# Second attention: transposes of the weights in two halves of 64 tokens

## The chip, the core and the metric

One core of a Trainium2 chip runs one program: two layers of gated cross attention and feed-forward (the second with 8 experts), on 2 x 1024 tokens of 256 channels in 32-bit floats, with 77 context keys. The metric is the device time of one execution in microseconds (us). TensorE (PE) multiplies and transposes and writes to PSUM, in 8 banks of 512 floats per partition; its weight loads are a row of their own (PEld). VectorE (DVE), ScalarE (ACT) and GpSimd (POOL) work beside it, and the engines wait for each other on semaphores.

## The reference

Of the reference the second attention matters here (16 heads of 16 channels, 77 keys; the second input is the context):

```
def _L1_xattn_ref(query, key, value, key_padding_mask, Wq, bq, Wk, bk, Wv, bv, Wo, bo, logit_scale, bias_table):
    ...
    q = proj(query, Wq, bq)
    k = proj(key, Wk, bk)
    v = proj(value, Wv, bv)
    ...
    scores = jnp.einsum('bhqd,bhkd->bhqk', q, k) * scale[None, :, None, None]
    scores = scores + _rel_bias(bias_table, tq, tk)[None]
    scores = jnp.where(key_padding_mask[:, None, None, :], neg, scores)
    attn = jax.nn.softmax(scores, axis=-1)
    out = jnp.einsum('bhqk,bhkd->bhqd', attn, v)
    ...
    out = out @ Wo + bo
    return out
```

Around it stand the first attention, a quantised feed-forward, and the expert layer; each result is added to x with a gate.

## The kernel before

The 2048 tokens are 16 tiles of 128. The second attention goes over them in pairs of tiles: t is the first tile of a pair, u (0 or 1) the tile in it, ci (0 or 1) the half of the heads (8 each). The order of each engine's work is written out by hand; nothing schedules it. Waits are on semaphores counted up by the other engines.

What TensorE does for a pair t, in `pair` of the `@block.tensor` section, is listed here with the names that the profile shows:

- `fill(t, ci)`: scores of 8 heads for both tiles into the four banks of `quad`. It is 16 products on four groups of 32 rows of the array (line 1657, `quad<-k_blockdiag,big_g`, 32x154). It waits for VectorE to be done with the scores before (`e_sub`).
- `weightsT(t, ci, u)`: takes the exponentials `e_` of 8 heads of one tile (in `big_g`) and transposes them, so that keys lie on partitions. Per head it is one transpose of 128 tokens x 77 keys (line 1950, `bank<-ident,big_g`, 128*77, 128x128: the weights are the exponentials, 128 rows and 77 columns, and the 128 columns of the identity are streamed). The first 4 heads go to bank 6, the other 4 to bank 7. Before the first four it waits for the exponentials (`e_exp`), and that ScalarE has copied out bank 6 of the call before; before the other four, that it has copied bank 7 (`pT_sb` counts the copies). A call follows another after one block of other work.
- `token_back(t - 2, u)`: 4 transposes of the heads' output back to tokens on partitions (line 1966, `heads_out`); `project_in`: 4 transposes of the attended tokens (line 1974); `project`: 8 products with the output weights (line 1657, `wo`); `queries(t + 2)`: 8 products (line 1657, `wq`).
- `heads(t, ci)`: 16 products of the values with the transposed weights `pT` (in `big_u`), on four column groups of 32 (line 1657, `bank<-big_u,v`, 77*32, 77x256). It waits for all copies of both tiles.

ScalarE copies each bank out (line 765, `big_u<-bank`, 77x512), so two copies of 512 elements a partition per call; it also makes the exponentials (line 990, in place) and copies queries (line 947), attended tokens (line 985) and `heads_out` (line 765). VectorE takes the maximum and subtracts it (lines 1487, 1488), for each ci and u; in the pairs near the diagonal of the distance bias (`t % TB == TB - NEAR`, t = 6 and 14) it first adds a bias (line 1485). It then makes `att` (lines 1453, 1454), adds the residual (1460) and takes its moments (1468 to 1474).

`PLACES` says where in `pT` each group of 4 heads lies. With ci = 0 these are groups 0 and 2, with ci = 1 groups 1 and 3. Bank 5 holds `oT`, bank 4 queries and projections, and bank 5 or 6 the output of `token_back`.

Of the kernel before, what the change touches and what calls it, by code (L numbers as in the profile page):

```python
# [17 lines left out]
P = 128  # L18
# [3 lines left out]
KEYS = 77  # L22
CH = D // P
H, HD = 16, 16
HK = H * KEYS
HQ = 4
HQK = HQ * KEYS
NQ = H // HQ
HC = H // CH
HCK = HC * KEYS  # L30
# [211 lines left out]
def flamingo_kernel(nc, a, out):  # L242
    ctx = ExitStack()
    with ctx:
        def sb(name, shape, dt=F32):
            return ctx.enter_context(nc.sbuf_tensor(name, shape, dt))
# [6 lines left out]
        pb = [quad[:, i, :] for i in range(4)] + [b[:, :] for b in bank]  # L253
# [15 lines left out]
        def part(reg, off, shape, dt=F32):  # L269

            n = int(np.prod(shape[1:]))
            words = n if dt in (F32, I32) else n // 2
            v = reg[0:shape[0], off:off + words]
            if dt != F32:
                v = v.bitcast(dt)
            if len(shape) == 3:
                v = v.rearrange("p (a b) -> p a b", a=shape[1])
            if len(shape) == 4:
                v = v.rearrange("p (a b c) -> p a b c", a=shape[1], b=shape[2])
            return v  # L280


        ident = sb("ident", [P, P])
# [7 lines left out]
        half = sb("half", [E, 1])  # L291
# [104 lines left out]
        e_ = part(BIGG, 8192, [P, 2, HK])  # L396
# [3 lines left out]
        pT = part(BIGU, 8192, [KEYS, H, 2 * P])  # L400
# [59 lines left out]

        LAST = NT - 2
        PLACES = (0, 2, 1, 3)

        def position(t):

            return t // TB * TB + (t - NEAR) % TB
# [19 lines left out]
        s = Signals(sem)  # L486
# [272 lines left out]
        def _(act):  # L759
            c = Chain(act, s.act_step)  # L760

            def copy(out_, in_, ready, n, done, **k):

                act.wait_ge(ready, n)
                act.activation(out_, in_, ACT.Copy, **k).then_inc(done, 1)  # L765
# [206 lines left out]


            def weightsT(t, ci, u):
                for k in range(2):
                    o = PLACES[2 * ci + k] * HQ
                    copy(pT[:, o:o + HQ, u * P:(u + 1) * P], pb[6 + k][0:KEYS, :].rearrange("k (h p) -> k h p", h=HQ),
                         s.pT_ps, 2 * (2 * t + 2 * ci + u) + k + 1, s.pT_sb)

            def heads_out(t, ci):  # L980
# [674 lines left out]
        def _(pe):  # L1655
            def mm(out_, lhsT, rhs, first, last):
                return pe.matmul(out_, lhsT=lhsT, rhs=rhs, start=first, stop=last)  # L1657
# [11 lines left out]
            for ci in range(CH):  # L1669
                for b in range(NB):  # L1670
                    o = (ci * NB + b) * KEYS
                    ins = pe.transpose(pb[0][:, o:o + KEYS], CTX[:, b, ci * P:(ci + 1) * P], ident[0:KEYS, 0:KEYS])
            ins.then_inc(s.ctxT_ps, 1)
            for dj in range(CH):
                for ci in range(CH):
                    ins = pe.transpose(pb[1][:, dj * D + ci * P:dj * D + (ci + 1) * P],
                                       WQ0[:, ci, dj * P:(dj + 1) * P], ident[:, :])
# [43 lines left out]
            for dj in range(CH):  # L1721
                ins = mm(pb[3][:, 320:320 + NB * KEYS], bq0[:, dj:dj + 1].to_broadcast([P, P]), K0T[:, dj, :],
                         dj == 0, dj == CH - 1)
# [81 lines left out]
            def weightsT(w, ps):  # L1805
                for k in range(4):
                    ins = pe.transpose(ps[:, k * P:(k + 1) * P], WF[:, src[4 * w + k]:src[4 * w + k] + P], ident[:, :])
                ins.then_inc(s.wT_ps, 1)
            pe.wait_ge(s.wq_sb, 1)
            pe.wait_ge(s.x1_done, NT)  # L1810
            for g in range(3):
                weightsT(3 + g, pb[g])
# [16 lines left out]
            with pe.Fori(0, NQB - 1) as q:  # L1829
                for j in range(FJ):  # L1830
                    block(0, q, j)
            pe.wait_ge(s.wq_sb, 3)
            weightsT(0, pb[6])
            for j in range(FJ):
                block(0, NQB - 1, j)
# [104 lines left out]
            def weightsT(t, ci, u):  # L1940
                n = 2 * t + 2 * ci + u
                pe.wait_ge(s.e_exp, n + 1)
                for k in range(2):
                    if n:
                        pe.wait_ge(s.pT_sb, 2 * (n - 1) + k + 1)
                    if (ci, u, k) == (1, 0, 0) and t:
                        pe.wait_ge(s.att_sb, t)
                    for h in range(HQ):
                        o = (2 * ci + k) * HQK + h * KEYS
                        ins = pe.transpose(pb[6 + k][0:KEYS, h * P:(h + 1) * P], e_[:, u, o:o + KEYS], ident[:, :])  # L1950
                    ins.then_inc(s.pT_ps, 1)

            def heads(t, ci):
                pe.wait_ge(s.pT_sb, 2 * (2 * t + 2 * ci + 1) + 2)
                for k in range(2):
                    for g in range(HQ):
                        h = (2 * ci + k) * HQ + g
                        ins = mm(pb[5][g * VE:(g + 1) * VE, k * 2 * P:(k + 1) * 2 * P], V1[:, t // TB * H + h, :],
                                 pT[:, PLACES[2 * ci + k] * HQ + g, :], True, True)
                ins.then_inc(s.oT_ps, 1)  # L1960
# [146 lines left out]
            for t in range(NT - 1):  # L2107
                n = NT - 1 - t
                ins = mm(pb[0][:, (t + 1) * E:NT * E].rearrange("p (t e) -> p t e", e=E), onesb[:, :],
                         OHB[:, t:t + 1, :].to_broadcast([P, n, E]), False, t == NT - 2)  # L2110
# [3 lines left out]
            for t in range(NT):  # L2114
                pe.wait_ge(s.at_row_sb, t // 4 + 1)
                ins = mm(pb[7][:, 0:WHERE * NS], AT_ROW[:, t, :], PLACE[:, t, :], t == 0, t == NT - 1)
# [3 lines left out]
            for t in range(NT):  # L2120
                ins = mm(pb[6][:, 0:(KINDS - WHERE) * NS], AT_ROW[:, t, :], SHARE[:, t, :], t == 0, t == NT - 1)
# [88 lines left out]
```

## Time and profile before

| | us |
|---|---|
| time, median of 3 runs | 461.93 (461.29 to 462.9) |
| time of the profiled execution | 460.87 |
| its span, first to last instruction | 459.1 |
| PE busy in it | 411.1 (90%) |
| DVE busy | 324.5 (71%) |
| ACT busy | 253.0 (55%) |
| POOL busy | 128.3 (28%) |
| PE at line 1950 (256 transposes) | 36.4 |
| ACT copies of line 765 into `big_u` (72) | 39.2 |
| granted TensorE clock, mean over the span | 0.943 |

The profiled execution's time is 1.8 us more than its span, and lies 1.1 us under the median. The second attention runs from about 226 to 326 us of the span. In the timelines below a row is a group of instructions of one kind: its start, how long from the first start to the last end, the engine, the line, what it writes from what it reads, its count, and in brackets idle time of the engine before it with what ended it. A matmul's time in such a row includes the way through the array, so matmuls overlap: 4 of them in 0.60 us, each 0.27 long, start every 0.11.

### The profile page before, as it was taken

To read this page: it belongs to the slowest core of one execution; us is meant where nothing else is said; L and a number is where in the kernel's file an instruction comes from. 1 tells how busy PE (TensorE), PEld (TensorE's weight loads), DVE (VectorE), ACT (ScalarE), POOL (GpSimd) and SP (SyncE) were. 2 spreads that over 40 slices of the span, in tenths; PEclk is the share of its full clock that TensorE was granted. 3 is DMA by queue.
4 is the path that set the end of the run, shared out by engine and by line. 5 is a ranking of instruction groups with operands and counts; after the bars stand their busy time and mean duration, and the time that the engine had idled before them with its cause. 6 is when DMAs were issued, how large, how long until landed. Compare 5 with 4: busy or idle time off the path is not lost.

```text
span 459.1 us, 7476 instructions
## 1 busy us (share of the span) xinstructions
PE 411.1 (90%) x2436; PEld 293.5 (64%) x2437; DVE 324.5 (71%) x660; ACT 253.0 (55%) x421; POOL 128.3 (28%) x143
## 2 busy tenths in 40 slices
PE   7998899999997129999999999997987999999993
PEld 7977644444445018878877768874866576767762
DVE  4999984369998999964776887778356465555652
ACT  3564655579998975412487767775541523424210
POOL 6523155000000440421196000100123645351222
PEclk9999999999996558999999999998897999999998
DMA  8910000000001004000399000000064312221000
GB/s 250 282 2 1 0 3 1 0 0 0 0 3 59 1 2 109 1 0 0 91 390 411 28 1 2 0 1 2 1 170 141 104 55 66 52 60 33 27 21 1
DMA packets 27424, 27.25 MB, mean 59 GB/s; under 512 B 11611, under 2 KB 23586, under 8 KB 27139
## 3 DMA queue, kind: packets, MB, share of 16 engines
q1 hardware_dynamic: 25187, 21.73, 15.3%
q0 software_dynamic: 2208, 5.14, 3.9%
q8 instruction: 17, 0.28, 0.3%
q14 instruction: 12, 0.10, 0.1%
HBM read 22.63 MB, written 5.15 MB: 61 GB/s over the span
## 4 chain that ended last, share of the span: by engine, by line
PE 58%; DVE 20%; issue 3%; ACT 3%; DMA 3%; POOL 2%; DVEq 0%; ACTq 0%; POOLq 0%
PE quad L1657 24%; PE bank L1657 23%; PE bank L1950 5%; DVE big_g L483 2%; DVE big_g L1391 2%; DVE amP L1365 2%; PE bank L2145 2%; DMA token_rows<-x_rows 2%; DVE mx L1487 2%; PE quad L1701 1%; DVE big_g L1485 1%; DVE big_g L1488 1%; DVE amZ L1301 1%; DVE amU L1307 1%; ACT big_u L765 1%
## 5 line engine op out<-in xcount | busy, mean ns | idle before, releaser
L1657 PE MATMUL quad<-yT,ffn_w 128*128 (+1 forms) x128 | 56.3, 593 | 0.0
L765 ACT ACTIVATE big_u<-bank 77x512 f32<-77x512 f32 (+2 forms) x72 | 39.2, 592 | 12.8 <-PE bank L1950 12.0
L1063 ACT ACTIVATE yT<-yT 128x512 f32<-128x512 f32 x23 | 14.5, 630 | 52.3 <-DVE yT L1612 52.3
L1657 PEld LDWEIGHTS quad<-yT,ffn_w 128*128 128x128 f32 x128 | 24.0, 190 | 29.5 <-issue 28.3
L1657 PE MATMUL quad<-big_g,yT 128*128 x92 | 41.8, 595 | 0.5 <-ACT yT L765 0.5
L1657 PE MATMUL bank<-big_u,yT 128*128 x184 | 41.8, 380 | 0.2 <-DVE yT L1626 0.2
L1950 PE MATMUL bank<-ident,big_g 128*77 128x128 f32 x256 | 36.4, 287 | 2.2 <-ACT big_g L990 1.9
L742 POOL DMA_INDIRECT out<-yT,k_blockdiag x23 | 23.3, 1015 | 50.7 <-DVE yT L1626 46.1
L1657 PEld LDWEIGHTS bank<-big_u,yT 128*128 128x128 f32 x184 | 34.1, 190 | 5.0 <-issue 0.9
L1612 DVE TENSOR_TENSOR yT<-quad,ffn_w 128x512 f32<-128x512 f32 x23 | 15.9, 692 | 25.5 <-PE quad L1657 25.5
L1950 PEld LDWEIGHTS bank<-ident,big_g 128*77 128x77 f32 x256 | 29.4, 153 | 7.1 <-ACT big_g L990 3.3
L1657 PE MATMUL quad<-ffn_w,big_u 128*128 128x256 f32 x144 | 31.6, 380 | 0.6 <-ACT big_u L765 0.6
L1657 PEld LDWEIGHTS quad<-ffn_w,big_u 128*128 128x128 f32 x144 | 27.2, 190 | 4.6 <-ACT big_u L765 0.8
L1657 PE MATMUL bank<-yT,ffn_w 128*128 (+1 forms) x64 | 28.8, 592 | 0.0
L990 ACT ACTIVATE big_g<-big_g 128x616 f32<-128x616 f32 x32 | 22.5, 722 | 11.0 <-DVE big_g L1488 11.0
L1657 PEld LDWEIGHTS quad<-big_g,yT 128*128 128x128 f32 x92 | 16.5, 190 | 16.7 <-issue 16.5
L626 POOL TENSOR_SCALAR ve<-mv 128x4 f32<-128x4 f32 (+3 forms) x7 | 1.7, 240 | 88.8 <-DVE mv L1474 84.8
L765 ACT ACTIVATE yT<-bank 128x512 f32<-128x512 f32 (+1 forms) x24 | 11.4, 525 | 25.5 <-PE bank L1701 17.3
L1256 DVE TENSOR_REDUCE amG<-big_g (+1 forms) x23 | 14.9, 682 | 14.8 <-ACT big_g L765 14.6
L1487 DVE TENSOR_REDUCE mx<-quad 128x8 f32<-128x616 f32 x24 | 19.0, 793 | 6.6 <-PE quad L1657 6.6
L659 POOL PARTITION_ALL_REDUCE scalars<-scalars x4 | 1.5, 366 | 74.7 <-DVE scalars L1346 44.0
L1657 PEld LDWEIGHTS bank<-yT,ffn_w 128*128 128x128 f32 x64 | 12.2, 190 | 15.3 <-issue 14.8
(318 smaller groups left out, 923.5 us busy)
## 6 DMA issues: line engine op xcount, KB each, us to landing
big_g<-in_L_ffn_W SPq DMA_DIRECT2D x1, 4096.0 KB, 13.4
big_u<-in_L_ffn_W SPq DMA_DIRECT2D x1, 4096.0 KB, 25.0
x_rows<-in_x SPq DMA_DIRECT2D x4, 512.0 KB, 5.8
ffn_w<-in_L_ffn_b SPq DMA_DIRECT2D x1, 2048.0 KB, 26.5
tmp<-bias_by_distance SPq DMA_DIRECT2D x2, 616.0 KB, 6.9
token_rows<-x_rows SPq DMA_DIRECT2D x1, 1032.0 KB, 10.6
tmp<-in_L_ffn_b SPq DMA_DIRECT2D x1, 1024.0 KB, 6.4
token_rows<-x_rows SPq DMA_DIRECT2D x1, 774.0 KB, 11.8
```

Source lines behind the costliest of these rows:

```text
L483: return eng.tensor_tensor(PR[h][:, :, q * QB:(q + 1) * QB], gated_int(q, h), up_int(q, h), ALU.mult)
L742: pool.indirect_dma_start(out.rearrange("b s d -> (b s) d"), bass.IndirectOffsetOnAxis(sid[:, t:t + 1], 0), res[:, t % 2, :], None, bounds ...
L765: act.activation(out_, in_, ACT.Copy, **k).then_inc(done, 1)
L990: act.activation(e8, e8, ACT.Exp).then_inc(s.e_exp, 1)
L1063: act.activation(hb[:, u, :], hb[:, u, :], ACT.Gelu).then_inc(s.gelu_sb, 1)
L1256: c.mark(dve.tensor_reduce(amG[:, ds(FJ * q + j, 1)], GT[:, j, ds(q * QB, QB)], AX.X, ALU.max, apply_absolute_value=True))
L1365: c.mark(dve.tensor_reduce(amP[:, 2 * q + h:2 * q + h + 1], PR[h][:, :, q * QB:(q + 1) * QB], AX.XY, ALU.max, apply_absolute_value=True))
L1391: ins = dve.tensor_scalar(GT[:, half(h), ds(o, n)], PR[h][:, :, ds(o, n)], sc[:, 20:21], MAGIC, ALU.mult, ALU.add)
L1487: c.link(dve.tensor_reduce(m8, s8, AX.X, ALU.max))
L1612: dve.tensor_tensor(hb[:, u, :], pb[2 + u], B1[:, ds(e * HID, HID)], ALU.add).then_inc(s.hb_sb, 1)
L1657: return pe.matmul(out_, lhsT=lhsT, rhs=rhs, start=first, stop=last)
L1950: ins = pe.transpose(pb[6 + k][0:KEYS, h * P:(h + 1) * P], e_[:, u, o:o + KEYS], ident[:, :])
```

## The change

In the second attention each transpose of 128 tokens x 77 keys becomes two of 64 tokens x 77 keys: tokens 0 to 63 on rows 0 to 63 of the array into bank 6, tokens 64 to 127 on rows 64 to 127 into bank 7. The two follow each other in the program, for each of the 8 heads. The streamed identity is its 64x64 block on the same rows, so 64 columns are streamed. A bank now holds 8 heads x 64 tokens, so both banks are complete only at the end of a call. The call waits for both copies of the call before, ahead of its first transpose. ScalarE still makes two copies of 77x512, now each with 2x4 pieces of 64 elements in place of 4 of 128.

```diff
@@ -460,6 +460,7 @@
         LAST = NT - 2
         PLACES = (0, 2, 1, 3)
+        HP = P // 2
@@ -972,9 +973,10 @@
             def weightsT(t, ci, u):
+                places = pT.rearrange("k (a c h) n -> k a c h n", a=2, c=CH)[:, :, ci, :, :]
                 for k in range(2):
-                    o = PLACES[2 * ci + k] * HQ
-                    copy(pT[:, o:o + HQ, u * P:(u + 1) * P], pb[6 + k][0:KEYS, :].rearrange("k (h p) -> k h p", h=HQ),
+                    o = u * P + k * HP
+                    copy(places[:, :, :, o:o + HP], pb[6 + k][0:KEYS, :].rearrange("k (a h n) -> k a h n", a=2, h=HQ),
                          s.pT_ps, 2 * (2 * t + 2 * ci + u) + k + 1, s.pT_sb)
@@ -1940,15 +1942,17 @@
             def weightsT(t, ci, u):
                 n = 2 * t + 2 * ci + u
                 pe.wait_ge(s.e_exp, n + 1)
-                for k in range(2):
-                    if n:
-                        pe.wait_ge(s.pT_sb, 2 * (n - 1) + k + 1)
-                    if (ci, u, k) == (1, 0, 0) and t:
-                        pe.wait_ge(s.att_sb, t)
-                    for h in range(HQ):
-                        o = (2 * ci + k) * HQK + h * KEYS
-                        ins = pe.transpose(pb[6 + k][0:KEYS, h * P:(h + 1) * P], e_[:, u, o:o + KEYS], ident[:, :])
-                    ins.then_inc(s.pT_ps, 1)
+                if n:
+                    pe.wait_ge(s.pT_sb, 2 * n)
+                if (ci, u) == (1, 0) and t:
+                    pe.wait_ge(s.att_sb, t)
+                for h in range(HC):
+                    o = ci * HCK + h * KEYS
+                    for k in range(2):
+                        half = slice(k * HP, (k + 1) * HP)
+                        ins = pe.transpose(pb[6 + k][0:KEYS, h * HP:(h + 1) * HP], e_[half, u, o:o + KEYS], ident[half, half])
+                        if h == HC - 1:
+                            ins.then_inc(s.pT_ps, 1)
```

On TensorE, in the half of a pair with ci = 0, from the fill to heads, before (a row is the line, the instruction, what it writes and reads, the shape of the output, the waits and the count):

```order
L1657 MATMUL quad<-k_blockdiag,big_g 128x154 x7
L1950 MATMUL bank<-ident,big_g 77x128 [waits pT_sb,e_exp]
L1950 MATMUL bank<-ident,big_g 77x128 x3
L1950 MATMUL bank<-ident,big_g 77x128 [waits pT_sb]
L1950 MATMUL bank<-ident,big_g 77x128 x3
L1966 MATMUL bank<-ident,heads_out 128x128 [waits oT_sb]
L1966 MATMUL bank<-ident,heads_out 128x128 x3
L1950 MATMUL bank<-ident,big_g 77x128 [waits pT_sb,e_exp]
L1950 MATMUL bank<-ident,big_g 77x128 x3
L1950 MATMUL bank<-ident,big_g 77x128 [waits pT_sb]
L1950 MATMUL bank<-ident,big_g 77x128 x3
L1657 MATMUL bank<-yT,wq 128x256 [waits y3T_sb]
```

The same place now (line numbers are a little higher in the changed program):

```order
L1659 MATMUL quad<-k_blockdiag,big_g 128x154 x7
L1953 MATMUL bank<-ident,big_g 77x64 [waits pT_sb,e_exp]
L1953 MATMUL bank<-ident,big_g 77x64 x15
L1970 MATMUL bank<-ident,heads_out 128x128 [waits oT_sb]
L1970 MATMUL bank<-ident,heads_out 128x128 x3
L1953 MATMUL bank<-ident,big_g 77x64 [waits pT_sb,e_exp]
L1953 MATMUL bank<-ident,big_g 77x64 x15
L1659 MATMUL bank<-yT,wq 128x256 [waits y3T_sb]
```

The blocks stand in the same order. A call is 16 instructions of half the columns in place of 8, and the wait in its middle is gone into the one at its start.

On ScalarE, the copies of the second half of a pair, before:

```order
L765 ACTIVATE big_u<-bank 77x4x128 [waits pT_ps] x2
L985 ACTIVATE big_g<-bank 128x512 [waits attT_ps]
L765 ACTIVATE big_u<-bank 77x4x128 [waits pT_ps] x2
L990 ACTIVATE big_g<-big_g 128x616 [waits e_sub] x2
L765 ACTIVATE heads_out<-bank 128x512 [waits oT_ps]
```

and now:

```order
L766 ACTIVATE big_u<-bank 77x2x4x64 [waits pT_ps] x2
L987 ACTIVATE big_g<-bank 128x512 [waits attT_ps]
L766 ACTIVATE big_u<-bank 77x2x4x64 [waits pT_ps] x2
L992 ACTIVATE big_g<-big_g 128x616 [waits e_sub] x2
L766 ACTIVATE heads_out<-bank 128x512 [waits oT_ps]
```

Order and counts are unchanged there; only the shape of the copies is another.

## Rows read from the trace of the kernel before

**Rows 1.** Chain of work that ended last, a half: start us, us, what.

```profile
269.27 0.81 PE quad L1657 x16
270.08 1.03 PE bank L1950 x8
...
275.32 0.73 PE quad L1657 x16
276.05 1.03 PE bank L1950 x8
```

**Rows 2.** The chain, half that starts at 232.8: ScalarE's last copies, then heads.

```profile
235.07 0.98 ACT big_u L765 x2
236.05 0.14 issue
236.18 1.07 PE bank L1657 x16
```

**Rows 3.** Timeline of PE, a half with queries: start us, us, engine, line, what.

```profile
300.61 1.10 PE L1950 MATMUL bank<-ident,big_g 128*77 128x128 f32 x8
301.55 0.60 PE L1966 MATMUL bank<-ident,heads_out 128*128 128x128 f32 x4
302.05 1.07 PE L1950 MATMUL bank<-ident,big_g 128*77 128x128 f32 x8
302.95 1.89 PE L1657 MATMUL bank<-yT,wq 128*128 128x256 f32 x8
304.68 0.60 PE L1966 MATMUL bank<-ident,heads_out 128*128 128x128 f32 x4
305.21 1.07 PE L1657 MATMUL bank<-big_u,v 77*32 77x256 f32 x16
```

**Rows 4.** Timeline of PE, a half with project; its last row is one instruction.

```profile
306.21 0.81 PE L1657 MATMUL quad<-k_blockdiag,big_g 32*128 32x154 f32 x16
306.95 1.10 PE L1950 MATMUL bank<-ident,big_g 128*77 128x128 f32 x8
...
309.29 0.45 PE L1657 MATMUL bank<-wo,big_g 128*128 128x256 f32 x1
```

**Rows 5.** Timelines of weight loads in three very short windows.

```profile
302.02 0.14 PEld L1950 LDWEIGHTS bank<-ident,big_g 128*77 128x77 f32 x1
...
306.21 0.19 PEld L1657 LDWEIGHTS quad<-k_blockdiag,big_g 32*128 32x128 f32 x2 [0.41 <-issue]
...
306.95 0.21 PEld L1950 LDWEIGHTS bank<-ident,big_g 128*77 128x77 f32 x2 [0.16 <-issue]
```

**Rows 6.** By line: duration ns min/median/max of one, first and last start us, forms.

```profile
L1657 PEld LDWEIGHTS quad<-k_blockdiag,big_g x236: 181/185/185, 225.8 to 312.6; 32*128 32x128 f32 x118
L1657 PE MATMUL quad<-k_blockdiag,big_g x240: 289/289/394, 225.7 to 312.7; 32*128 32x154 f32 x120
...
L1950 PEld LDWEIGHTS bank<-ident,big_g x256: 143/148/253, 226.5 to 324.6; 128*77 128x77 f32 x128
L1950 PE MATMUL bank<-ident,big_g x256: 272/273/465, 226.5 to 324.8; 128*77 128x128 f32 x128
```

**Rows 7.** Timeline of ACT: the first copy of a call alone, and both.

```profile
301.31 0.59 ACT L765 ACTIVATE big_u<-bank 77x512 f32<-77x512 f32 x1 [0.70 <-PE bank L1950]
...
301.31 1.08 ACT L765 ACTIVATE big_u<-bank 77x512 f32<-77x512 f32 x2 [0.70 <-PE bank L1950]
```

**Rows 8.** First pair of near tiles: PE's timeline, a row of the chain, PE's timeline.

```profile
258.92 1.96 PE L1657 MATMUL bank<-wo,big_g 128*128 128x256 f32 x8
...
261.54 0.76 DVE x_rows L1460 x2
...
267.15 1.07 PE L1657 MATMUL bank<-big_u,v 77*32 77x256 f32 x16
269.27 0.81 PE L1657 MATMUL quad<-k_blockdiag,big_g 32*128 32x154 f32 x16 [1.05 <-DVE big_g L1488]
```

**Rows 9.** Timeline of PE, the tail.

```profile
317.61 1.23 PE L1657 MATMUL bank<-big_u,v 77*32 77x256 f32 x16 [1.28 <-DVE big_g L1454]
320.70 1.96 PE L1950 MATMUL bank<-ident,big_g 128*77 128x128 f32 x8 [1.86 <-ACT big_g L990]
...
325.01 1.14 PE L1701 MATMUL quad<-ident,x_rows 128*128 128x128 f32 x8
```

**Rows 10.** Windows: us, busy (count) of PE, PEld, DVE, ACT, POOL, then PEclk, DMA, GB/s.

```profile
264.00:270.00 6.00, 4.95 (x53) 3.71 (x52) 5.64 (x10) 3.59 (x8) 0.00 (x0) 1.00 0.00 0
...
321.00:324.00 3.00, 3.00 (x16) 3.00 (x15) 0.00 (x0) 1.74 (x4) 0.00 (x0) 0.50 0.00 0
```

## The prediction

> **What bounds the kernel now.** I read four views: the chain of work that ended last, to find which engine sets the pace of the second attention (about 226 to 326 us); the timeline of TensorE there, block by block; the timelines of weight loads and of ScalarE, for what lies between two blocks; and the busy time by windows, for the granted clock.
>
> The chain runs through TensorE alone for most of the stage: fill, transposes, small transposes, transposes, matrix products, one after the other without a gap [rows 1]. I call the piece of work from one fill to the next a half: a first call of weightsT (8 heads, one tile of tokens), a block of 4 small transposes, a second call, then queries or project, token_back in some, and heads. The chain is TensorE's in ten halves, those whose first call starts at 232.8, 237.9, 244.3 and 250.2, and at 270.0, 276.0, 282.3, 288.3, 294.6 and 300.6. Between them lies a pair of near tiles in which VectorE has one more pass per unit and TensorE waits 1.05 us for it at 269.27 [rows 8]; the last pair (307 to 320) is of that kind too, and the first half (226.5) ends in a wait for VectorE. So what matters is what a half costs TensorE, ten times, and what the tail does.
>
> **The transposes themselves.** Four transposes with 128 moving columns take 0.60 us of which the last is 0.272 long: they start (0.60 - 0.27)/3 = 0.109 us apart [rows 3, 6]. A call has 8, so the eighth starts some 0.83 us after the first load. The weights of the next one load meanwhile. Two loads of 77 columns take 0.21 us together and one is 0.148 long, so they are 0.065 apart: the load is not the limit at 0.109 [rows 5, 6].
>
> The change streams 64 columns per instruction, on rows 0 to 63 and 64 to 127 in turn. Do two row groups run side by side? No transposes do here before, but the fill does so with four groups of 32 rows: two of its loads take 0.19 together at 0.181 each, so they start within 0.01 us, and its 16 products with 154 columns are done in 0.81 us [rows 4 to 6], where 16 one after the other at the rate of the transposes (0.109/128 per column) would take 2.1 us. I take it that two halves run side by side too, a pair costing as much as one of them. Its stream is then about 0.056 us, half of 0.109, but its load still has 77 columns, so 0.065 a pair and 0.52 us for a call's 8 pairs, instead of 0.87. The bounds are 0.056 (the load hidden somehow) and 0.130 (the row halves one after the other). The Trainium skill, "TensorEngine Tiling (Array Packing)", Theoretical Speedup, gives up to 2x where the small dimension is 64 or less; that would be 0.44 us a call and take 1.6 us off the sum below. The measured gap of two 77-column loads speaks against the full 2x.
>
> **The wait that is added.** Before, bank 6 is complete after four transposes: ScalarE starts its copy 0.70 us after the first load [rows 3, 7], and the second call needs only that one copy to begin (bank 7 is asked for later). With the change both banks fill in step and the second call waits for both copies. A matmul of 128 columns is 0.272 long and one of 154 is 0.289, so one of 64 is about 0.218 (estimate, 0.84 ns per column) [rows 6]. Counted from the first load: the eighth pair starts at 0.065 + 7 x 0.065 = 0.52; it ends at 0.74; ScalarE starts at 0.78 (0.04 after the end, as now: 3 x 0.109 + 0.065 + 0.27 + 0.04 = 0.70). Two copies take 1.08 [rows 7], so both banks are free at 1.86. TensorE goes on 0.11 after a copy it waits for: the first copy ends at 301.31 + 0.59 = 301.90, the next load is at 302.02 [rows 5, 7]. The second call so loads at 1.97; now it is at 1.41. The block of 4 transposes between them (0.44) was what filled this time before; it can't fill 1.4 us. The copies write four-dimensional pieces of 64 instead of 128 elements, which I price at nothing: their 512 elements a partition are the same.
>
> **The switch.** When the row or column split of the array changes, the next load waits for the running stream and about 0.09 more: fill to call, last start 306.73 plus its stream 0.13, next load 306.95; token_back to heads, 305.01 plus 0.11, next 305.21 [rows 3, 4, 5]. From one block of full transposes to the next nothing is lost. Before, the calls had the same split as the blocks around them, so a half has three switches; now each edge of a call is one. Those around the small block are hidden in the wait for ScalarE. The one after the second call is not: 0.09, and a load of 128 columns (0.11) that could run ahead before and can't now.
>
> **A half, summed.** From the first load to the stream of queries or project: 1.97 + 0.52 (eighth pair) + 0.06 (its stream) + 0.09 + 0.11 = 2.74 us. Before, 302.95 - 300.61 = 2.34 with queries [rows 3], and 309.29 - 306.95 + 0.07 (the first product of project is 0.45 long, not 0.38, as its load was not ahead) = 2.41 with project [rows 4]. So **+0.40** and **+0.33**. The gain of 0.31 per call is real, but in the first call it only makes TensorE wait longer, and in the second the switch takes most of it.
>
> The half at 232.8 is dearer: there heads waits for ScalarE's last copies already [rows 2]. First load 232.81; second 234.78; copies done 234.78 + 0.78 + 1.08 = 236.64; heads at 236.76 instead of 236.18: **+0.58**.
>
> First stretch: 0.58 + 0.40 + 0.33 + 0.40 = 1.71. Second: 3 x 0.40 + 3 x 0.33 = 2.19. Halves at 256.6 and 262.5: +0.73 against an idle time of 1.05 before the fill, hidden [rows 8]; VectorE's residual needs project, which ends at 260.88 and would end at 261.2, against its own start at 261.54, so VectorE does not move either. The last pair is hidden likewise.
>
> Tail: the calls at 320.70 and 323.30 run at a granted clock of 0.50, the 1.2 GHz level [rows 10]. There a transpose costs (1.96 - 0.42)/7 = 0.22 [rows 9], a pair 0.13. First call's copies start 1.39 after the load, end at 2.47, second load 2.58, eighth pair 1.04 later, stream 0.11, switch and load about 0.39: next stream near 324.8, now 325.01. **-0.2**.
>
> Sum: 1.71 + 2.19 - 0.2 = +3.7 us. The profiled execution took 460.87 us (span 459.1 and 1.8 around it), which gives 464.6; it lies 1.1 under the median 461.93 of the runs, so for the median **465.6**. All terms are in the span; nothing after 326 us depends on more than the time at which the tail ends.
>
> **Rivals.**
> *The array gives all of it (not slower).* Place: the edges of each call. If a pair costs its 0.056 stream alone, and the switch costs nothing because each row half frees its own rows, then both banks are copied at 1.79, the second load is at 1.90, the next stream at 2.42: +0.08 and 0 per half. With +0.45 for the first half: 0.45 + 0.16 + 3 x 0.08 = 0.85, tail -0.5, so +0.3, 462.2. It decides once the other nine halves cost 0.15 or less each, since the sum then stays within 1.4. Against it: both kinds of switch in the rows cost 0.09, and the load's 0.065 is measured. For it: no switch between 64 and 128 rows is in the trace.
> *The halves take turns.* Transposes might not pair as products do. A call then takes 16 x 0.065 = 1.04: copies from 1.23 on, second load 2.42, next stream 3.72: +1.4 and +1.3 per half, some 13.6 for the ten with the first at 1.5, and 1.6 past what the near tiles hide, with the tail about 478. Against it: the fill's loads, within 0.01.
> *The clock drops more.* TensorE gains idle times of 0.6 to 0.8 us in each half. Now the clock holds 1.00 through the 1.05 us gap [rows 10] and falls to 0.50 only after gaps of 1.28 and 1.86 us near 317 to 321 [rows 9]. If it also fell near 268, or earlier in the last pair, some 3 us of work there would take up to twice as long: 2 to 3 us more, 468.
> *The clock stays up in the tail.* First call to next stream would take 2.74 instead of 4.1, and y4_in 0.3 less: 463.9.
>
> **Chances.** Forecast 0.63; array gives all 0.12; turns 0.08; clock drops more 0.09; clock stays up 0.06; 0.02 for something else. The range 462.1 to 468.6 takes in all but the turns and what I have not thought of. A measurement of this kernel can tell about 0.3% (1.4 us) from no change. Slower by more than that: forecast, turns, both clock cases, less the edge of the latter and part of what is unknown, 0.83. Within: mostly the second case, 0.13. Faster: that case with the clock up as well, 0.04.
>
> **What would show it.** The profile after should have: in a TensorE-bound half, 16 transposes in about 0.74 us (about 0.01 and 0.06 between starts by turns), ScalarE's first copy 0.78 after the first load, the second call 1.97 after it with TensorE idle 0.5 to 0.8 us before it and ScalarE named as releaser; queries 2.7 after the first load; TensorE's share below 90% though its span grew. The near tiles' fill should still wait for VectorE, some 0.3 us. Starts 0.065 apart without pairs would show the turns; a second call near 1.4, or queries near 2.4, would make the forecast wrong on the other side; and a total far from the sum of ten halves would mean that something in the tail or its clock moved.

## The result, and the profile after

| | kernel before, us | changed kernel, us |
|---|---|---|
| median, runs beside each other | 461.61 (461.11 to 462.9, 4 runs) | 470.6 (468.43 to 471.9, 4 runs) |
| ratio | | 1.0185, 95% interval 1.0163 to 1.0206 |
| profiled execution | 460.87, span 459.1 | 470.96, span 469.2 |
| granted TensorE clock, mean | 0.943 | 0.933 |

The change made the kernel 9.0 us slower, where I had forecast 3.7, in a range that ended 7 us above. In two further groups of runs the difference was 4.9 and 10.3 us (469.9 against 465.03, 471.89 against 461.55). Two executions of e11 below were slow (467.78 and 622.47 us, at mean clocks of 0.915 and 0.647): its ratio leaves them out, its median of 462.1 holds them and would be 461.6 without them.

The chain of work that ended last, in the changed kernel. It answers to [rows 1]; a row is start us, us, what.

```profile
281.73 0.73 PE quad L1659 x16
282.46 0.74 PE bank L1953 x16
283.20 1.07 ACT big_u L766 x2
284.28 0.14 issue
284.41 0.77 PE bank L1953 x16
285.18 1.92 PE bank L1659 x8
```

The small transposes that followed the first call in the chain are gone from there; in their place stand ScalarE's two copies. In the stretch read (281 to 296 us) the chain goes from TensorE to ScalarE and back in each half. The timelines of TensorE and ScalarE in the same half answer to [rows 3, 7], the loads to [rows 5], and the durations by line to [rows 6].

```profile
281.66 0.81 PE L1659 MATMUL quad<-k_blockdiag,big_g 32*128 32x154 f32 x16
282.39 0.76 PE L1953 MATMUL bank<-ident,big_g 64*77 64x64 f32 x16
283.09 0.66 PE L1970 MATMUL bank<-ident,heads_out 128*128 128x128 f32 x4
284.41 0.77 PE L1953 MATMUL bank<-ident,big_g 64*77 64x64 f32 x16 [0.67 <-ACT big_u L766]
...
288.47 0.81 PE L1659 MATMUL quad<-k_blockdiag,big_g 32*128 32x154 f32 x16
```

```profile
283.19 1.08 ACT L766 ACTIVATE big_u<-bank 77x512 f32<-77x512 f32 x2 [0.80 <-PE bank L1953]
285.18 1.08 ACT L766 ACTIVATE big_u<-bank 77x512 f32<-77x512 f32 x2 [0.92 <-PE bank L1953]
```

```profile
289.20 0.14 PEld L1953 LDWEIGHTS bank<-ident,big_g 64*77 64x77 f32 x2 [0.16 <-issue]
...
289.20 0.21 PEld L1953 LDWEIGHTS bank<-ident,big_g 64*77 64x77 f32 x4 [0.16 <-issue]
...
L1953 PEld LDWEIGHTS bank<-ident,big_g x512: 140/146/249, 228.8 to 332.2; 64*77 64x77 f32 x171
L1953 PE MATMUL bank<-ident,big_g x512: 213/229/388, 228.8 to 332.3; 64*77 64x64 f32 x171
```

A call of 16 transposes takes 0.76 to 0.77 us where 8 took 1.07 to 1.10. Two loads on the two row halves take 0.14 together, as long as one; four take 0.21. So the halves do run side by side, a pair every 0.07. The first copy starts 0.80 after the call's start (0.78 forecast), takes 1.08 with the second, and the second call's first transpose is at 284.41, 2.02 after the first call's (1.97 to its load forecast), behind 0.67 us of idle time. In each half of 281.66 to 308.04 the same is seen: from fill to fill 6.81 us with queries (6.34 before) and 6.38 with project (5.97 before).

Where the 10.1 us between the two spans lie, by the starts of the fills in both profiles: +2.2 before the second attention begins (fill at 218.74 and 220.98), +1.7 in the first half (fill at 232.07 and 236.04), +4.7 in the ten TensorE-bound halves and the near pair between them, which adds 0.01 (to the fill at 306.21 and 314.85), +1.3 in the last pair and the tail (to the first product with `gm`, where the expert layer's routing begins, at 332.58 and 342.56), and +0.1 after it. The first, second and fourth are places with a lower granted clock. The program before the second attention is the same in all kernels here; over the fourteen profiles its fill lies between 218.74 and 220.98, and the kernel before has the earliest, so the +2.2 is not the change's. By windows (us, busy of the engines, then PEclk, DMA, GB/s), these are stretches of the changed kernel, with most of the ten halves as the third; those of before are 1.00 at 38:42 and 226:236, and 0.76 in 317:331:

```profile
38.00:42.00 4.00, 4.00 (x15) 3.36 (x14) 3.66 (x14) 0.49 (x1) 1.45 (x3) 0.50 0.00 0
...
231.00:235.00 4.00, 4.00 (x28) 2.78 (x29) 3.18 (x7) 1.68 (x3) 2.43 (x2) 0.60 0.98 368
...
252.00:315.00 63.00, 56.80 (x736) 41.73 (x736) 47.12 (x96) 44.18 (x82) 1.91 (x2) 1.00 0.06 25
...
333.00:338.00 5.00, 5.00 (x20) 3.84 (x22) 0.10 (x1) 1.90 (x4) 0.00 (x0) 0.54 0.01 3
```

And TensorE's timeline at two of them. Eight products of queries take 3.48 us instead of 1.89 behind an idle time of 1.26; in the tail project takes 3.54, where it took 1.89 in the kernel before.

```profile
230.79 0.77 PE L1953 MATMUL bank<-ident,big_g 64*77 64x64 f32 x16 [1.26 <-ACT big_u L766]
231.49 3.48 PE L1659 MATMUL bank<-yT,wq 128*128 128x256 f32 x8
...
329.34 0.77 PE L1953 MATMUL bank<-ident,big_g 64*77 64x64 f32 x16 [2.02 <-ACT big_g L992]
...
334.32 3.54 PE L1659 MATMUL bank<-wo,big_g 128*128 128x256 f32 x8
```

So two questions for the chip: is the loss per half really the wait for both copies and not the narrow transposes, and what is the rest.

### The profile page after: what moved, and what is told of

Read it like the earlier page. It is cut to its first block, busy times and chain, and to the rows that moved or that the text cites. A ratio compares the mean times of both kernels' runs of the same rounds, so it can differ in the third digit from the quotient of the medians.

```text
span 469.2 us, 7988 instructions
## 1 busy us (share of the span) xinstructions
PE 412.6 (88%) x2692; PEld 290.7 (62%) x2693; DVE 325.2 (69%) x660; ACT 253.7 (54%) x421; POOL 128.2 (27%) x143
## 4 chain that ended last, share of the span: by engine, by line
PE 63%; DVE 21%; ACT 5%; issue 4%; POOL 2%; DMA 2%; SPq 1%; DVEq 0%; POOLq 0%; ACTq 0%
PE bank L1659 26%; PE quad L1659 26%; PE bank L1953 4%; ACT big_u L766 3%; DVE big_g L484 2%; DVE big_g L1393 2%; DVE amP L1367 2%; PE bank L2149 2%; PE quad L1703 2%; DMA gates<-in_g_ffn 1%; DVE mx L1489 1%; DVE big_g L1487 1%; DVE big_g L1490 1%; DVE amZ L1303 1%; DVE amU L1309 1%
## 5 line engine op out<-in xcount | busy, mean ns | idle before, releaser
L1953 PE MATMUL bank<-ident,big_g 64*77 64x64 f32 x512 | 25.1, 237 | 13.3 <-ACT big_u L766 11.2
L1953 PEld LDWEIGHTS bank<-ident,big_g 64*77 64x77 f32 x512 | 21.1, 148 | 19.5 <-issue 16.4
L1659 PEld LDWEIGHTS quad<-ffn_w,big_u 128*128 128x128 f32 x144 | 27.2, 190 | 4.7 <-ACT big_u L766 0.8
## 6 DMA issues: line engine op xcount, KB each, us to landing
ffn_w<-in_L_ffn_b SPq DMA_DIRECT2D x1, 2048.0 KB, 26.4
token_rows<-x_rows SPq DMA_DIRECT2D x1, 1032.0 KB, 10.3
```

The costliest lines, as they stand in the source:

```text
L1953: ins = pe.transpose(pb[6 + k][0:KEYS, h * HP:(h + 1) * HP], e_[half, u, o:o + KEYS], ident[half, half])
```

## Experiments: the wait or the transposes

Each group of kernels was timed beside the kernel before, on chip 14 (B and D) and chip 12 (C).

| group, medians | before | kernels beside it |
|---|---|---|
| B | 465.03 | e1 469.9, e2 464.62, e3 468.57, e4 470.38 |
| C | 461.43 | e5 469.65, e6 462.41, e7 461.76, e8 461.04 |
| D | 461.55 | e9 471.89, e10 467.1, e11 462.1, e12 460.73 |

In group B the kernel before itself is 3.5 us slower than in the other two, so differences are compared within a group only.

**e1, the changed kernel again.** No edit.

> The changed kernel once more, for a second profile and more clocks. Its first profile has three things beside what I forecast: the granted clock at half near 38 to 41 us, long before the changed part (worth some 2 us), at half for one stretch in the first half of the second attention (231.5 to 234.5, 1.7 us), and later in the tail than before (2.4 us given up between 329 and 338 against the times at full clock). Theory A (wait plus clock): each TensorE-bound half costs 0.40 to 0.48 us more again, to the last 0.05, since it is a fixed chain of copies; the rest of the 8.9 us is clock and varies, so the times of the runs should fall with their mean clock, about 470.5 at 0.933 and 468.5 at 0.943, and the first-half drop should be there again, because TensorE idles 1.5 us between the two calls there. Theory B (all array): halves cost more than 0.45 and times do not follow the clock.

Measured: 469.9 (469.35 to 474.06), ratio 1.0117 (1.0083 to 1.0151). The halves took 6.81 and 6.38 again. The low clock before the attention was not there, the first half had none, but two halves later there was a longer one (238.2 to 248.4). Windows and TensorE's timeline:

```profile
240.00:248.00 8.00, 7.79 (x51) 6.23 (x48) 3.78 (x6) 3.02 (x6) 7.92 (x2) 0.50 1.08 385
...
243.92 3.78 PE L1659 MATMUL bank<-yT,wq 128*128 128x256 f32 x8
```

That half took 10.69 us instead of 6.81; before the clock fell, TensorE had idled 1.25, 0.67 and 0.64 us within 10 us. This was the slowest of the six runs, 474.06 with a mean clock of 0.933; four lay at 469.35 to 469.93 with 0.940 to 0.957. These four are 4.3 to 4.9 above the median of before. That is near the 4.7 of the ten halves, but they have no trace, so it is not shown that the halves are all of it. The times did not follow the mean clock as neatly as I expected (469.93 at 0.957, 469.35 at 0.940), since the mean also counts stretches in which TensorE has nothing to do.

**e2, only the first call of a half in halves of 64 tokens.**

```diff
+            def weightsT(t, ci, u):
+                (weightsT_halves if u == 0 else weightsT_whole)(t, ci, u)
```

with `weightsT_halves` the changed kernel's and `weightsT_whole` the former one, on TensorE and on ScalarE.

> Only the first call of each half is made in halves of 64 tokens; the second call transposes whole tiles as before, so it can start when one bank is copied. Theory A (the wait for both copies is the cost, with the switch behind the second call): first copy 0.80 after the first load, second load 1.51 after it (1.41 before, 1.99 in the changed kernel), queries 2.45 (2.34 before): +0.10 us for each of ten halves, +1 us in all; near 462.5 with no clock loss in the first half. Rival (the narrower transposes cost by themselves, in each call alike): half of the changed kernel's loss, about +4.5, 466.

**e3, only the second call.** The same with `u == 1`.

> Only the second call of each half is made in halves of 64 tokens; the first transposes whole tiles as before. Theory A: the second call must wait for both copies of the first, 0.70 + 1.08 + 0.11 = 1.89 after the first load, then 0.83 to the next stream: queries 2.72 (+0.38), project +0.30, the half at 232.8 +0.5: +3.6 us in all without clock loss, 465.2, and up to 3 more by the clock, as TensorE idles 0.5 to 0.9 us in each half as in the changed kernel. Rival (both calls alike): about +4.5 with no difference to the run with the first call.

Measured: e2 464.62, ratio 1.0004 (0.9984 to 1.0024); e3 468.57, ratio 1.0075 (1.0053 to 1.0096). TensorE's timelines of a half with project, in e2 and then of one with queries in e3:

```profile
284.13 0.76 PE L1962 MATMUL bank<-ident,big_g 64*77 64x64 f32 x16
284.82 0.66 PE L2003 MATMUL bank<-ident,big_g 128*128 128x128 f32 x4
285.66 1.07 PE L1976 MATMUL bank<-ident,big_g 128*77 128x128 f32 x8 [0.18 <-ACT big_u L766]
```

```profile
280.61 0.77 PE L1962 MATMUL bank<-ident,big_g 64*77 64x64 f32 x16 [0.38 <-ACT big_u L766]
281.30 1.99 PE L1668 MATMUL bank<-yT,wq 128*128 128x256 f32 x8
```

e2 is 0.4 us under its kernel before where +1 was expected, and its interval (-0.7 to +1.1 us) holds both; the trace decides here. In e2 the second call starts 1.53 after the first (1.41 to 1.44 before), the halves take 6.44 and 6.07: +0.10 each, as the wait for one copy says. In e3 they take 6.71 and 6.28: +0.37 and +0.31, against +0.38 and +0.30 expected, and the total is 3.5 us over for 3.6. The same narrow transposes cost 0.10 in one place and 0.3 to 0.4 in the other, where both copies must be waited for and full-width products follow. The two together, 0.47 and 0.41, are the changed kernel's loss per half. The rival of equal shares is out.

**e4, the row halves one after the other, each bank waited for alone.**

```diff
+                for k in range(2):
+                    if n:
+                        pe.wait_ge(s.pT_sb, 2 * (n - 1) + k + 1)
                     ...
+                    for h in range(HC):
+                        o = ci * HCK + h * KEYS
+                        ins = pe.transpose(pb[6 + k][0:KEYS, h * HP:(h + 1) * HP], e_[half, u, o:o + KEYS], ident[half, half])
+                    ins.then_inc(s.pT_ps, 1)
```

> All calls in halves of 64 tokens, but first the eight transposes on rows 0 to 63 into bank 6, then the eight on rows 64 to 127 into bank 7, so that the banks are done one after the other as before and each is waited for alone; nothing runs side by side. A pace of one 77-column load, 0.065, gives a call 1.04 us (0.55 in the changed kernel, 0.87 before). Theory A: first copy 0.79, second load 1.50, next stream 2.80 after the first load: +0.46 with queries, +0.39 with project, about as the changed kernel, although the array's gain is gone: +4.0 us, with TensorE busy where it idled, so with less clock loss: 466. Rival (what counts is how fast the array does the transposes): slower than the changed kernel by 0.5 us per call, 475 or more.

Measured: 470.38, ratio 1.0118 (1.0088 to 1.0149), the same as the changed kernel; halves of 6.73 and 6.29, 0.08 to 0.09 shorter than the changed kernel's. TensorE's timeline:

```profile
284.77 1.09 PE L1953 MATMUL bank<-ident,big_g 64*77 64x64 f32 x16
285.80 0.66 PE L1977 MATMUL bank<-ident,big_g 128*128 128x128 f32 x4
286.38 1.09 PE L1953 MATMUL bank<-ident,big_g 64*77 64x64 f32 x16
```

With calls of 1.09 us, 0.32 longer than the changed kernel's, a half is no slower: the second call starts 0.41 us earlier (1.61 after the first, 2.02 there), which pays for its 0.32 and leaves the 0.08. The length of the first call is hidden in the wait; that of the second is not. The call is shorter than the 15 x 0.069 + 0.23 = 1.27 of sixteen transposes in turn, though, so my premise that nothing runs side by side was not met: see the last section. And the total did not come out 4 us above the kernel before but 5.4, with the tail's low clock the longest of the group (tail 22.17 us from last fill to first gm product).

## Experiments: the clock

**e5, the changed kernel with idle products; e6, the kernel before with them in the tail.** Products of the identity whose result nobody reads (the kernel's own function `idle_work`, which it uses elsewhere), on a PSUM bank that is free there. The edit of e5 is shown; e6 has the last two places of it, with 8 and 16.

```diff
                 weightsT(t, 0, 0)
+                if t == 0:
+                    idle_work(pb[5], 8)
                 ...
                     token_back(t - 2, 1)
+                    if t == LAST:
+                        pe.wait_ge(s.x3_done, LAST - 2)
+                        idle_work(pb[4], 4)
                     pe.wait_ge(s.att_sb, t - 1)
                 ...
+            idle_work(pb[4], 16)
             weightsT(LAST, 1, 0)
```

> The changed kernel with idle products (128 columns of the identity, result unused) where TensorE waits longest: 8 between the two calls of the first half, 4 before the last pair's heads and 16 before the tail's first call, all in time that was idle. Theory A (part of the loss is the clock that falls after idle time): no half-rate stretch near 231 nor in the tail from 329 to 338; the stretch from the last fill to the first product with gm takes 18 to 19 us (21.3 and 20.9 in the two profiles of the changed kernel), the first halves 6.5 and 6.0; the total falls by 2 to 4 us against the changed kernel on the same chip and stays above the kernel before, as the ten halves still cost 4.7 more. Rival (the clock falls by chance or by the kind of work, whatever idles): no change, within 1 us of the changed kernel, with the same half-rate stretches.

> The kernel before with idle products in the tail only: 8 before the last pair's heads and 16 before its first call. Theory A: the tail's half-rate stretch (318.3 to 325.7, some 5 us of work in it) goes or shrinks, last fill to first product with gm 18.3 to 18.8 us instead of 20.4: 1.5 to 2 us faster than the kernel before. Rival: no change within 0.7 us.

Measured: e5 469.65, ratio 1.0178 (1.0152 to 1.0204), 8.2 us over the kernel before, with no changed kernel beside it to tell the 2 to 4 us expected; e6 462.41, ratio 1.0044 (1.0016 to 1.0073), slower rather than faster. Windows over the whole second attention, e5 and e6:

```profile
226.00:345.00 119.00, 107.15 (x1379) 80.78 (x1377) 81.49 (x173) 79.19 (x148) 23.32 (x12) 1.00 0.25 91
...
226.00:340.00 114.00, 111.17 (x1133) 87.52 (x1131) 81.49 (x173) 78.88 (x149) 24.34 (x15) 1.00 0.27 97
```

The clock held 1.00 from end to end, in both. But the products overran the gaps, as the timeline of e6 shows:

```profile
320.19 3.84 PE L1657 MATMUL bank<-ident 128*128 128x128 f32 x32
323.87 1.04 PE L1950 MATMUL bank<-ident,big_g 128*77 128x128 f32 x8
```

Sixteen products are 32 instructions and take 3.84 us in a gap of some 2. So the tail took 20.28 us in e6 and 20.65 in e5 all the same, e5's first half 7.20 instead of 6.54 at the full clock, and the totals say nothing yet: the expected gains were missed. They were repeated with fitting counts (e10, e11).

**e9, the changed kernel a third time; e10, with 4 idle products between the calls of the first half and 8 before the tail's first call; e11, the kernel before with 4 before the last pair's heads and 8 before the tail's first call.** The edits are those of e5 and e6 with these counts.

> The changed kernel a third time, as the measure for the three beside it on the same chip. Its ten halves must again take 6.82 and 6.38 us where the clock is full (4.7 us more in all than before), and its total the kernel before plus 4.7 plus what the clock takes: 5 to 9 more.

> The changed kernel with idle products that just fit the idle time: a product of 32-bit floats turned out to be two instructions, 0.24 us, so the 8 and 16 of the run before overran the gaps by 0.6 and 1.9 us. Now 4 between the two calls of the first half and 8 before the tail's first call. Theory A (idle time lets the clock fall, and that is the rest of the loss): no half-rate stretch between 226 and 345, the tail (last fill to first gm product) 18.5 to 19.0 us instead of about 21, 2 to 4 us faster than the changed kernel on this chip, and 3 slower than the kernel before. Rival (the clock falls as often, elsewhere): same as the changed kernel within 1 us.

> The kernel before with fitting idle products in the tail: 4 before the last pair's heads, 8 before the tail's first call. Theory A: tail 18.4 to 18.8 us instead of 20.4, 1.5 to 2 us faster than the kernel before. Rival (no gain from the clock): within 0.7 us.

Measured: e9 471.89 (467.45 to 474.44), ratio 1.0225 (1.0184 to 1.0266); e10 467.1 (464.66 to 468.8), ratio 1.0114 (1.0084 to 1.0143); e11 462.1, ratio 1.0004 (0.9981 to 1.0028). TensorE in the tail, of e9 and of e10, and the windows over it:

```profile
323.79 1.91 PE L1659 MATMUL bank<-big_u,v 77*32 77x256 f32 x16 [0.18 <-DVE big_g L1456]
326.88 1.30 PE L1953 MATMUL bank<-ident,big_g 64*77 64x64 f32 x16 [1.17 <-ACT big_g L992]
...
322.00:334.00 12.00, 9.81 (x77) 7.26 (x74) 4.56 (x9) 6.82 (x12) 0.00 (x0) 0.58 0.00 1
```

```profile
324.09 2.05 PE L1659 MATMUL bank<-ident 128*128 128x128 f32 x16
326.13 0.77 PE L1953 MATMUL bank<-ident,big_g 64*77 64x64 f32 x16
...
226.00:260.00 34.00, 30.30 (x423) 22.59 (x421) 23.32 (x48) 25.11 (x47) 19.35 (x5) 1.00 0.84 310
318.00:336.00 18.00, 15.63 (x187) 12.32 (x183) 10.46 (x30) 10.46 (x20) 1.75 (x4) 1.00 0.01 2
```

The idle products end with the gap and the clock stays up; the tail takes 18.31 us, against 21.05 in e9, 20.85 in e1 and 21.33 in the changed kernel's first profile. The median falls by 4.8 us on the same chip, with six executions each and ranges that overlap between 467.45 and 468.8. That is more than the 2 to 4 expected, and more than the traces account for: they show 2.7 in the tail and nothing in the first half, where e9 kept the full clock without idle products. The rival, that the clock falls as often elsewhere, is out for this stretch: in every profile without idle products in the tail there is a half-rate stretch in it (before, changed, e1, e2, e3, e4, e7, e9), and in none of the six with them (e5, e6, e8, e10, e11, e12). It is not out for the whole program: behind the attention e10 has 13.6 us at half rate (350.1 to 356.9 and 360.3 to 367.1), e9 6.8, and their profiled executions differ by 1.6 us only.

This table gives the spans of six profiles by stage, in us, from the starts of the fills (the second column ends where the first half begins):

| | to first half | first half | ten halves and near pair | last pair and tail | behind first gm product |
|---|---|---|---|---|---|
| before | 225.7 | 6.35 | 74.1 | 26.4 | 126.5 |
| changed | 228.0 | 8.07 | 78.8 | 27.7 | 126.6 |
| e1 | 226.2 | 6.54 | 82.9 | 27.2 | 129.3 |
| e9 | 227.1 | 6.54 | 78.8 | 27.4 | 128.6 |
| e10 | 226.2 | 6.54 | 79.0 | 24.7 | 130.6 |
| e11 | 226.2 | 6.35 | 74.1 | 24.3 | 126.6 |

e10 against e11 is the change at a full clock from 226 us to the first gm product: 0.2 in the first half, 4.8 in the ten, 0.4 in the last pair and tail, 5.4 us in all. Their medians differ by 5.0. The last column is the same program in every kernel, and it falls into two groups over the fourteen profiles: 126.4 to 127.0 (before, changed, e5, e6, e7, e8, e11) and 128.6 to 130.6 (e1 to e4, e9, e10, e12). So up to 4 us of any difference between two single executions can come from there.

In e11 the tail takes 18.27 us against 20.39, yet the median is that of the kernel before: the 1.5 to 2 us expected were missed. Its runs fall into two groups, 459.3 to 459.7 (four) and 461.6 and more. Windows in e11's profile (459.3) and in e12's (463.35) where the experts' first products stand, and their timelines, show one place where such a difference arises:

```profile
353.00:361.00 8.00, 6.65 (x24) 3.39 (x23) 2.07 (x3) 4.22 (x9) 6.17 (x7) 1.00 0.40 106
...
354.93 3.69 PE L1657 MATMUL quad<-big_g,yT 128*128 x8 [0.53 <-ACT yT L765]
```

```profile
354.00:362.00 8.00, 6.77 (x11) 2.91 (x12) 0.69 (x1) 3.02 (x7) 5.87 (x8) 0.57 0.38 104
...
356.33 6.34 PE L1668 MATMUL quad<-big_g,yT 128*128 x8 [0.28 <-issue]
```

The same eight products cost 3.69 or 6.34 us as the clock is up or down while they run, which is 2.6 of the 3.8 us between the two profiles behind the first gm product. That may be where the tail's gain goes again in the slower group. It is not shown: the executions of that group have no trace.

## Experiments: work for the wait

**e7, transposes in halves only where ci = 0, and queries split around the second call; e8, with idle products in the tail as in e5; e12, with fitting ones (2 and 8).**

```diff
+            def weightsT(t, ci, u):
+                (weightsT_whole if ci else weightsT_halves)(t, ci, u)
                 ...
-                weightsT(t, 0, 1)
                 if t == 2:
                     pe.wait_ge(s.y3T_sb, 12)
                 if 4 <= t < LAST:
                     pe.wait_ge(s.x3_done, t - 2)
                 if t < LAST:
-                    queries(t + 2)
+                    queries(t + 2, (0,))
+                weightsT(t, 0, 1)
+                if t < LAST:
+                    queries(t + 2, (1,))
```

> Halves of 64 tokens only where ci = 0, and there the queries are split: 4 of their 8 products stand before the second call, in the time in which it waits for both copies; where ci = 1 whole tiles are transposed as before. Theory A (the wait is what eats the gain): the second call now loads 2.16 after the first, when both copies have just been made, nothing waits, and heads begins 4.36 after the first load (4.60 before, 5.08 in the changed kernel): halves with queries 6.1 us (6.34 before, 6.82 changed), those with project 5.98 as before. Five of them on the path: 1.2 us faster than the kernel before. Rival (narrow transposes and their switches cost whatever they lie beside): halves with queries 6.34 or more, same as before or slower.

> The kernel with split queries and the idle products of the tail (4 before the last pair's heads, 16 before the tail's first call). Theory A: both gains add, 2.5 to 3 us faster than the kernel before, 0.6%. Rival: the idle products delay the tail or leave the clock as it is, no more than 1.2 us.

> Split queries, and fitting idle products (2 before the last pair's heads, 8 before the tail's first call). A half with queries took 6.23 us there (6.34 before), so 0.6 us from five of them, and the tail's gain with it: 2 to 2.5 us faster than the kernel before. Rival: within 0.7 us.

Measured: e7 461.76, ratio 1.0001 (0.9986 to 1.0015); e8 461.04, ratio 0.9994 (0.9981 to 1.0008); e12 460.73, ratio 0.9977 (0.9949 to 1.0005). The timeline of TensorE in a half of e7:

```profile
290.15 0.76 PE L1963 MATMUL bank<-ident,big_g 64*77 64x64 f32 x16
...
291.34 1.03 PE L1668 MATMUL bank<-yT,wq 128*128 128x256 f32 x4
292.30 0.77 PE L1963 MATMUL bank<-ident,big_g 64*77 64x64 f32 x16
293.00 1.13 PE L1668 MATMUL bank<-yT,wq 128*128 128x256 f32 x4
...
294.49 1.07 PE L1668 MATMUL bank<-big_u,v 77*32 77x256 f32 x16
```

The idle time before the second call is gone, and heads begins 4.34 after the first call (4.60 before, 5.08 changed; 4.36 expected). The next fill follows 1.16 after heads instead of 1.00, so a half takes 6.23, not 6.10: still 0.11 less than before and 0.58 less than the changed kernel. The fill waits for ScalarE's copies of the queries (`q_sb`): in e7 they run from 294.68 to 295.51, behind an exponential, and the fill starts at 295.65; in the same half of the kernel before they ended at 293.41 and the fill started at 293.90. Five such halves are 0.6 us, less than a median of this kernel tells, and the forecast of 1.2 was missed. So was the 2.5 to 3 of e8, whose overlong idle products left the tail at 20.07 us. e12, with a tail of 18.25 us, is 0.8 us under the kernel before by its median, where 2 to 2.5 were expected; its interval includes no change, so no version was shown to beat the kernel before.

## Why the prediction was wrong, point by point

- *TensorE bounds the stage in ten halves; the near tiles hide their share.* Right. The near pair's fill waited for VectorE (0.18 us left of 1.05, some 0.3 forecast), and the pair as a whole is 0.01 us longer.
- *Pairs run side by side, limited by the load.* Right in the pace: 0.069 a pair, 0.065 forecast. That the load and not something else sets it is argued from its 0.065; no run changed the load alone.
- *The wait for both copies.* Right in kind and size: second call at 2.02 for 1.97, and e2 and e3 put it where I had.
- *The half, summed: +0.40 and +0.33.* Under-sized by 0.07 each: 0.47 and 0.40 measured. The eighth pair starts at 0.54 instead of 0.52, in both calls; a 64-column matmul is 0.229 long, not 0.218; after the second call the next load comes 0.10 after the stream's end. The half at 232.8 cost 0.64 for 0.58. The ten halves cost 4.7, for 3.9 forecast.
- *The first half, priced at nothing.* Wrong, and with +1.7 the largest miss that belongs to the change. I let its wait hide in the wait for VectorE, which had 0.31 us to spare, and never worked out the idle time between its two calls: no small transposes stand there, so it grew from 0.34 to 1.26 us. At the full clock that costs 0.19 (6.54 for 6.35 in e1, e9 and e10); the other 1.5 in the changed kernel's profile is queries at half rate.
- *The tail, -0.2.* Wrong: +1.3. I counted the calls at the old clock and let the clock come back when it had. In the changed kernel the half-rate stretch was as long as before, 6.8 us, but lay elsewhere: 330.8 to 337.6, where before it was 318.4 to 325.2. So the first call ran at full rate and `x_rows` began 1.1 us sooner than before, counted from the fill at 314.85 (306.21), and then `x_rows` and project at half rate cost 2.4.
- *The rival "the clock drops more", 0.09 and 2 to 3 us.* In kind this is what came on top of the forecast, but not where I had put it: the clock held near the first near pair in all three profiles, and in the last pair it fell later than before in the changed kernel's first profile and in e1, earlier only in e9. The new half-rate stretch lay in the first halves in 2 of 3 profiles (231.8 to 235.2, and 238.2 to 248.4 in e1). The step that failed is the sum's premise that the clock stays where it was: the forecast kept the clock of the kernel before in the first half and in the tail. I had also read the rows too kindly. The idle time of 1.86 us ended at 320.70, but the window 318:321 of the kernel before has a clock of 0.57 already and 314:318 has 1.00, so there it fell behind the gap of 1.28 alone; the first half's new gap is as long.
- Another 2.2 us of the profiled difference lie before the second attention, where TensorE's program is the same; no term of the forecast was meant for it. e7's profile has the same low clock there (0.53 in 37:44) and e1's has not. It comes and goes in kernels of both kinds, and is not the change's.
- *Why a fall comes when it does.* Open. The gaps of 0.67 us in each of the ten halves left the clock at 1.00 from 252 to 315 in all three profiles. The gap of 1.26 us in the first half was followed by a fall 1.0 us later in the changed kernel's profile; the same gap of 1.25 in e1 and e9 was not; in e4 the clock fell at 322.7 behind gaps of 0.35 and 0.65, ahead of the long one. No run shows a length of gap that decides.

The other rivals fell: the array did not give all, the row halves did not take turns, and the clock did not stay up in the tail. The sum at an undisturbed clock is borne out better than the total says: 5.4 us in e10 against e11, of which the forecast had 3.9 in the ten halves.

## What to carry to other kernels

When an operation is made faster between two engines that hand buffers to each other, write down when each buffer is full and when it is free again before counting what the operation saves. Here 0.33 us less per call bought 0.6 us more of waiting, because two half-filled banks are as good as none to the engine that empties them. And where the bounding engine is TensorE, new idle time can cost twice: once as itself, and again as half-rate work behind it. So work out the new idle time of every stage, those priced at nothing too, and look at the longest ones: the regular gaps of 0.67 us cost only themselves from 252 us on, the single one of 1.26 cost 1.5 us more in one profile of three. Keep the stages that the change does not touch apart, too: here they moved by up to 4 us from one execution to another.

## What the runs showed of the hardware that I had not expected

- Transposes on different row halves overlap even when the program does not interleave them. In e4 eight on rows 0 to 63 stand before eight on rows 64 to 127. The second eight start 0.33 us after the first, whose last starts at 0.53, each eight at its own 0.069; the 16 take 1.09 us, where in turn they would take about 1.27.
- A plain product of 32-bit floats appears as two instructions of 128 columns (16 idle products are 32 rows, 3.84 us, 0.24 each), a transpose of the same shape as one (0.109).
- Twelve idle products, of no use to the result, kept the clock at 1.00 in the tail and took 2.7 us off it (e10 against e9); the medians of the two are 4.8 us apart, of which the traces explain no more than that.
